# Adding a pooling's two sums to a stored chunk by accumulating transfers from GpSimd

## The reference, cut to what matters

```python
def layer0(x, indices, fc1_w, fc1_b, fc2_w, fc2_b, experts_w, experts_b):
    h = gelu(einsum('bnd,hd->bnh', x, fc1_w) + fc1_b)              # exact gelu
    shared = einsum('bnh,sh->bns', h, fc2_w) + fc2_b               # 384 columns
    expert_x = einsum('bnh,bph->bnp', h, experts_w[indices]) + experts_b[indices][:, None, :]
    return concatenate([shared, expert_x], axis=-1)                # 512 columns

def layer1(hidden, W1, b1, v, prompt_type_ids):
    scores = einsum('bsa,a->bs', tanh(hidden @ W1 + b1), v)
    # per batch: mask l <= j (type 0), l >= j (type 1) or l != j (type 2)
    p = softmax(where(mask, scores[:, None, :], -1e30), axis=-1)
    return einsum('bjl,bld->bjd', p, hidden) / mask.sum(-1)[..., None]

x = x + layer0(x, ...)
x = x + layer1(x, ...)
```

## Time and profile before

| | before |
|---|---|
| median of 3 runs | 1356.64 us (1356.3 to 1356.75) |
| the profiled execution's own time | 1356.64 us |
| its span, first to last instruction | 1354.8 us |
| TensorE busy | 1347.6 us (99%) |
| VectorE busy | 1230.8 us (91%) |
| ScalarE busy | 866.6 us (64%) |
| GpSimd busy | 0.2 us |
| moved by transfers | 62.98 MB |
| mean granted clock of TensorE | 1.000 of full speed |

### The profile page before, as it was taken

One profiled execution on the slowest core, in us unless ns is written; L12 is line 12 of the kernel. 1 busy time (PEld: TensorE's weight loads), 2 busy tenths in 40 slices (PEclk: granted clock), 3 DMA queues, 4 the chain that ended last, 5 costly groups with the idle time before them and its releaser, 6 DMA issues.

```text
span 1354.8 us, 22001 instructions
## 1 busy us (share of the span) xinstructions
PE 1347.6 (99%) x8734; PEld 874.3 (65%) x8734; DVE 1230.8 (91%) x2057; ACT 866.6 (64%) x1493; POOL 0.2 (0%) x4
## 2 busy tenths in 40 slices
PE   9999999999999999999999999999999999999998
PEld 5458476584856758476584756748567584765856
DVE  7988889899898999989899898998989899898998
ACT  4868748376593856848377583756838468483753
POOL 0000000000000000000000000000000000000000
PEclk9999999999999999999999999999999999999999
DMA  8410020110201102011110201102021020200001
GB/s 294 150 48 22 0 71 24 48 48 1 78 17 63 32 8 79 9 62 32 45 50 1 79 17 55 41 0 78 17 63 32 13 77 6 71 24 15 25 10 55
DMA packets 29192, 62.98 MB, mean 46 GB/s; under 512 B 5922, under 2 KB 6690, under 8 KB 26658
## 3 DMA queue, kind: packets, MB, share of 16 engines
q1 hardware_dynamic: 28658, 61.05, 13.7%
q10 hardware_dynamic: 432, 0.53, 0.1%
HBM read 44.79 MB, written 16.78 MB: 45 GB/s over the span
## 4 chain that ended last, share of the span: by engine, by line
PE 96%; DVE 4%; ACT 0%; issue 0%; DVEq 0%
PE ps L398 15%; PE ps L399 15%; PE ps L400 15%; PE ps L317 14%; PE ps L319 14%; PE ps L318 14%; PE ps L430 1%; PE ps L288 1%; PE ps L435 1%; PE ps L598 1%; PE ps L299 1%; PE ps L303 1%; PE ps L301 1%; PE ps L426 1%; PE ps L425 1%; PE ps L424 1%
## 5 line engine op out<-in xcount | busy, mean ns | idle before, releaser
L400 PE MATMUL ps<-hl,w2h 128*128 128x512 f16 x768 | 291.0, 379 | 0.0
L399 PE MATMUL ps<-hh,w2h 128*128 128x512 f16 x768 | 291.0, 379 | 0.0
L398 PE MATMUL ps<-hh,w2l 128*128 128x512 f16 x768 | 291.0, 379 | 0.0
L317 PE MATMUL ps<-xh,w1h 128*128 128x256 f16 x960 | 261.7, 273 | 0.0
L318 PE MATMUL ps<-xl,w1h 128*128 128x256 f16 x960 | 261.7, 273 | 0.0
L319 PE MATMUL ps<-xh,w1l 128*128 128x256 f16 x960 | 261.7, 273 | 0.0
L650 ACT ACTIVATE g<-ps,b1s,ds 128x512 f32<-128x512 f32 x240 | 173.4, 773 | 99.0 <-PE ps L319 99.0
L317 PE MATMUL ps<-xh,ch 128*128 128x256 f16 x720 | 196.4, 273 | 0.0
L319 PE MATMUL ps<-xh,cl 128*128 128x256 f16 x720 | 196.3, 273 | 0.0
L318 PE MATMUL ps<-xl,ch 128*128 128x256 f16 x720 | 196.2, 273 | 0.0
L1064 DVE SCALAR_TENSOR_TENSOR hl<-g,ix,hh 128x512 f16<-128x512 f32 x244 | 179.2, 747 | 1.6
(11 more groups left out here) (208 smaller groups left out, 2348.4 us busy)
## 6 DMA issues: line engine op xcount, KB each, us to landing
xr<-in_xT SPq DMA_DIRECT2D x62, 256.0 KB, 3.1
er<-in_ew SPq DMA_DIRECT2D x15, 1024.0 KB, 6.3
out<-xr SPq DMA_DIRECT2D x60, 256.0 KB, 2.4
raw<-in_w SPq DMA_DIRECT2D x28, 256.0 KB, 6.1
er<-in_w SPq DMA_DIRECT2D x3, 1024.0 KB, 10.1
xr<-in_ew SPq DMA_DIRECT2D x1, 1024.0 KB, 6.2
out<-er SPq DMA_DIRECT2D x3, 256.0 KB, 2.5
xr<-in_xT ACTq DMA_DIRECT2D x2, 256.0 KB, 5.1
```

Source lines behind the costliest of these rows:

```text
L317: mm(to, wh, mh, start=i in (1, 5) and c == 0, stop=False, skip_group_check=True)
L398: mm(po(b, o), wl, hh[:, k, :], start=False, stop=False, skip_group_check=True)
L399: mm(po(b, o), wh, hh[:, k, :], start=False, stop=False, skip_group_check=True)
L400: m = mm(po(b, o), wh, hl[:, k, :], start=False, stop=k == NH - 1, skip_group_check=True)
```

## The change

Of the nine steps of a chunk the last two, the additions on VectorE, are gone, so a batch's pooling has 52 steps. The chunk is stored as soon as it is scaled. GpSimd gets a program: when a chunk's store has landed and the first sum's row is ready, it issues a transfer of this row to the output with an addition in the transfer (511 of the 512 columns, one column shifted), waits until it has landed, and issues the second row's in the same way. Chunks 1 and 3 use the rows `zFi` and `zB` instead of `cp` and `cq`. The products of chunk 2 wait until the transfers of chunk 0 have read their rows (their landing is waited for), those of chunk 3 for chunk 1's; the steps of the next batch's weight rows that write `cp`, `zFi` and `zB` wait for chunks 2 and 3. The counts of `pool` change so that the second layer's part still issues 35 steps, the first layer's part 17 instead of 25; in the tail 47 steps stand ahead of the maxima and none behind the sums.

```diff
--- before.py
+++ after.py
@@ -210,6 +210,8 @@
          "el", "hl", "bound", "sums", "sumsl", "pads", "masks", "combos", "xl", "add0", "add1", "x2l", "awll", "pool",
          "shift", "nl", "scan", "tailmax", "neg", "plow", "pairsum", "wsum", "rz", "outrdy"))
 
+    first_added, second_added = sem("firstadd"), sem("secondadd")
+
 
     def x_loaded(b):
         return 16 * (b // XB + 1)
@@ -262,13 +264,23 @@
     def ds2_value(b, o):
         return 4 + 2 * b - (o == 3) if b else (1, 2, 4, 3)[o]
 
-    ROWS, STEPS = 13, 60
+    ROWS, STEPS = 24, 52
 
     def pool_value(b, step):
         return STEPS * b + step
 
-    def chunk_pooled(b, c):
-        return pool_value(b, ROWS + 11 + 9 * (c + 1))
+    def chunk_scaled(b, c):
+        return pool_value(b, ROWS + 7 * c + 5)
+
+    def first_ready(b, c):
+        return pool_value(b, ROWS + 7 * c + 6)
+
+    def second_ready(b, c):
+        return pool_value(b, ROWS + 7 * c + 7)
+
+    def pooled_rows(c):
+
+        return ((cp, cq), (zFi, zB[:, 0:S]))[c % 2]
 
 
     def tensor_program(eng):
@@ -1212,8 +1224,13 @@
             stt(ga, mBx, cB[:, i], mt, ALU.add, ALU.subtract).then_inc(pool_step)
             yield
             e.wait_ge(io_in, 16)
+            if b:
+                e.wait_ge(first_added, 16 * nth_chunk(b - 1, 2))
             ts(cp, io[:, :], cntq[:, i], cntp[:, i], ALU.mult, ALU.add).then_inc(pool_step)
             yield
+            if b:
+                e.wait_ge(first_added, 16 * nth_chunk(b - 1, 3))
+                e.wait_ge(second_added, 16 * nth_chunk(b - 1, 3))
             if b < LAST - 1:
                 e.wait_ge(exp_done, b + 1)
             else:
@@ -1249,32 +1266,30 @@
             tt(ga, ga, mt, ALU.mult).then_inc(pool_step)
             yield
             for c in range(KD):
-                x, n = chunk(b, c), done + 24 + 9 * c
-                e.wait_ge(pool_step, n - 1 if c else n)
-                tt(cp, wF, x, ALU.mult).then_inc(pool_step)
+                x, n = chunk(b, c), done + ROWS + 7 * c
+                first, second = pooled_rows(c)
+                e.wait_ge(pool_step, n - 7 if c > 1 else n)
+                if c > 1:
+                    e.wait_ge(first_added, 16 * nth_chunk(b, c - 2))
+                tt(first, wF, x, ALU.mult).then_inc(pool_step)
                 yield
-                e.wait_ge(pool_step, n)
-                tt(cq, wB, x, ALU.mult).then_inc(pool_step)
+                if c > 1:
+                    e.wait_ge(second_added, 16 * nth_chunk(b, c - 2))
+                tt(second, wB, x, ALU.mult).then_inc(pool_step)
                 yield
                 e.wait_ge(pool_step, n + 1)
-                scan(cp, aF, cp, 0.0, ALU.mult, ALU.add).then_inc(pool_step)
+                scan(first, aF, first, 0.0, ALU.mult, ALU.add).then_inc(pool_step)
                 yield
                 e.wait_ge(pool_step, n + 2)
-                scan(back_of(cq), back_of(aB), back_of(cq), 0.0, ALU.mult, ALU.add).then_inc(pool_step)
+                scan(back_of(second), back_of(aB), back_of(second), 0.0, ALU.mult, ALU.add).then_inc(pool_step)
                 yield
                 stt(x, be, 1.0, x, ALU.add, ALU.mult).then_inc(pool_step)
                 yield
                 e.wait_ge(pool_step, n + 3)
-                tt(cp[:, 0:S - 1], cp[:, 0:S - 1], al[:, 1:S], ALU.mult).then_inc(pool_step)
+                tt(first[:, 0:S - 1], first[:, 0:S - 1], al[:, 1:S], ALU.mult).then_inc(pool_step)
                 yield
                 e.wait_ge(pool_step, n + 4)
-                tt(cq[:, 1:S], cq[:, 1:S], ga[:, 0:S - 1], ALU.mult).then_inc(pool_step)
-                yield
-                e.wait_ge(pool_step, n + 6)
-                tt(x[:, 1:S], x[:, 1:S], cp[:, 0:S - 1], ALU.add).then_inc(pool_step)
-                yield
-                e.wait_ge(pool_step, n + 8)
-                tt(x[:, 0:S - 1], x[:, 0:S - 1], cq[:, 1:S], ALU.add).then_inc(pool_step)
+                tt(second[:, 1:S], second[:, 1:S], ga[:, 0:S - 1], ALU.mult).then_inc(pool_step)
                 yield
 
         pools = itertools.chain.from_iterable(pooling(b) for b in range(LAST))
@@ -1402,7 +1417,7 @@
 
         for b in range(1, B):
 
-            takes = ((0, 3, 1), (1, 1, 1), (1, 2, 1), (1, 2, 0), (1, 2, 0), (2, 2, 0))
+            takes = ((0, 2, 1), (1, 1, 0), (1, 1, 1), (1, 1, 0), (0, 1, 0), (1, 1, 0))
             if b == 1:
                 takes = ((0, 0, 0),) * 5 + ((1, 1, 1),)
             for c, (one, two, three) in zip(range(2, PAIRS), takes):
@@ -1495,7 +1510,7 @@
         natural_low(1, 1)
         pool(3 + 4 + 3 + 4)
         natural_low(2, 2)
-        pool(4 + 2)
+        pool(2)
         e.wait_ge(score_done, LAST + 1)
         e.wait_ge(own_done, 1)
         scan(mF[:, 1:1 + HALF], pad, pf[3][:, 0:HALF], -BIG, ALU.max, ALU.max).then_inc(scan_step)
@@ -1525,7 +1540,6 @@
         e.wait_ge(pair_sums, 2)
         tt(be, be, mt, ALU.add).then_inc(weights_sum)
         ts(rz[:, :], lcol[:, :], cntq[:, i], cntp[:, i], ALU.mult, ALU.add).then_inc(rz_step)
-        pool(4)
         e.wait_ge(totals_done, 1)
         e.wait_ge(rz_step, 1)
         tt(rz[:, :], pf[0][:, 0:4], rz[:, :], ALU.mult).then_inc(rz_step)
@@ -1562,7 +1576,7 @@
             dma(expert_rows(b), ew[bass.ds(n, 1), :, :].rearrange("a p n -> p (a n)")).then_inc(e_loaded(b)[0], 16)
 
         def store(b, c):
-            e.wait_ge(pool_step, chunk_pooled(b, c))
+            e.wait_ge(pool_step, chunk_scaled(b, c))
             dma(out[b, :, c, :], chunk(b, c)).then_inc(x_out[b % XB * KD + c], 16)
             if b + XB < B:
                 load_x(b + XB, c)
@@ -1614,6 +1628,20 @@
             stores = (B - 1 - i // KD) // XB + 1 + (i == LAST % XB * KD + 3)
             e.wait_ge(s, 16 * stores)
 
+
+    def gpsimd_program(eng):
+        e = Engine(eng)
+        for b in range(LAST):
+            for c in range(KD):
+                first, second = pooled_rows(c)
+                e.wait_ge(x_out[b % XB * KD + c], x_stored(b))
+                e.wait_ge(pool_step, first_ready(b, c))
+                eng.dma_start(out[b, :, c, 1:S], first[:, 0:S - 1], accum_op=ALU.add).then_inc(first_added, 16)
+                e.wait_ge(first_added, 16 * nth_chunk(b, c))
+                e.wait_ge(pool_step, second_ready(b, c))
+                eng.dma_start(out[b, :, c, 0:S - 1], second[:, 1:S], accum_op=ALU.add).then_inc(second_added, 16)
+        e.wait_ge(second_added, 16 * nth_chunk(LAST - 1, 3))
+
     with nc.Block() as block:
         @block.sync
         def _(eng):
@@ -1630,6 +1658,10 @@
         @block.vector
         def _(eng):
             vector_program(eng)
+
+        @block.gpsimd
+        def _(eng):
+            gpsimd_program(eng)
 
 
 def kernel(x, itok_B_0_15, itok_B_0_2, L0_cond_fc1_w, L0_cond_fc1_b, L0_cond_fc2_w, L0_cond_fc2_b,
```

## The result

The changed kernel takes 1390.11 us (median of 6 runs, 1385.36 to 1393.11) against 1356.70 us of the kernel before beside it: ratio 1.0244, 95% interval 1.0228 to 1.026. It is slower by 33 us, where 1357.9 was forecast and 1380 was the end of the range. The profiled execution took 1393.11 us, the slowest of the six, and its span is 1391.3, so what follows is about 36.5 us of span.

What follows compares the result with a forecast made beforehand. TensorE was taken to bound the loop, leaving nothing to gain there. In the tail, 2.67 us less VectorE work against a 4.0 us stall put the scan 1.3 later: 1356.64 + 1.3 = 1357.9 us, range 1355.3 to 1380.

Steps and rivals of the forecast that it cites:

- What bounds the kernel: Loop: TensorE is busy for all 82.00 us of a batch's period, so relieving VectorE there gains nothing.
- What the tail can give: Tail: at most 1.2 us, because the scan ahead of the maxima needs the second half's scores, whose matmuls end at 1332.61.
- The price of one transfer: GpSimd's accumulating transfer: a plain store and two passes more, 4.6 us, between 2.4 and 6.6.
- thresholds of 5.1 and 5.0: Loop: transfer times above which TensorE notices the waits for chunk 0's (5.1 us) and chunk 1's sums (5.0).
- L: Time from the wait that lets GpSimd issue one accumulating transfer to its landing, taken as 4.6 us.
- The upper bound, 6.6: One accumulating transfer: load of the old output, a store and one more pass of the data, 6.6 us in all.
- The wait in the tail: Tail: VectorE stalls 4.0 us once, ahead of chunk 2's second product; the scan before the maxima starts 1.3 us later.
- the rule (2L - 5.2): Tail: VectorE's stall before chunk 2's second product, two transfer times less 5.2 us; 4.0 us at 4.6 each.
- The waits in the loop: Loop: chunks 2 and 3 wait for the transfers of chunks 0 and 1; both hidden at 4.6 us a transfer.
- rival C: Loop: transfers over 5.0 us make chunk 3's second product, behind the expert's load, delay pair 3's `add_second`; 1372 to 1386; 0.36.
- Rival D: Loop: GpSimd's issuing disturbs VectorE, 0.5 us a batch beyond its slack, 7 us, 1364; chance 0.04.
- B: Whole kernel: a transfer costs about a plain store, up to 3.3 us; 1355.4 to 1355.5; chance 0.10.

Runs made afterwards that it cites:

- e1: Changed kernel with rows of its own for each chunk, so no row is reused too early; all 120 transfers stay: 1354.89 us, ratio 0.9985.
- e7: Kernel before, with accumulating transfers and rows of their own only in batch 14's pooling in the tail, eight transfers: 1354.65 us, ratio 0.9984.
- e4: Kernel before, no GpSimd transfers, plus four useless VectorE additions ahead of pair 1's `add_second` in 14 batches: 1391.01 us, ratio 1.0251.
- e3: Changed kernel with the store of chunk 1 ahead of the expert's load in SP's queue: 1384.41 us (one run).
- e5: Kernel with rows of its own for each chunk, but in the loop chunk 3 reuses chunk 1's rows and waits for its transfers: 1365.65 us.
- e6: Kernel with rows of its own for each chunk, but in the loop chunk 2 reuses chunk 0's rows and waits for its transfers: 1378.19 us.
- e2: Changed kernel with the same transfers without the addition, so the sums overwrite what the store left; all waits stay: 1358.2 us (one run).
- e9: Changed kernel with the first sum added on VectorE again before the store, one transfer per chunk instead of two: 1358.51 us, ratio 1.0009.

## Why the prediction was wrong, point by point

**What bounds the kernel: right.** The loop had nothing to give: e1 and e7 have equal times with and without VectorE's relief there, and e4 shows the other half, that lateness at that place is paid in full.

**What the tail can give: right, a little more came.** The bound of 1.2 us was argued from the second half's score, and in e1 TensorE's first matmul with the exponentials starts 1.2 us earlier, counted from the last `stt`. Another 0.4 lies behind TensorE's last matmul (3.1 us to the end in place of 3.6), where I had costed the four steps removed behind the sums at nothing: before, VectorE's last four scalings of 512 columns ran directly behind one another from 1348.56, held up by these steps, and five output transfers were issued within 3 us; in e1 they are spread over 4. That those steps are the cause was not tested by itself. The rest of the 1.9 us of span (2.2 in e7) is 0.2 to 0.5 ahead of the loop.

**The price of one transfer: this is the step that failed.** The term "a plain store and two passes more, 2.4 + 2 x 1.1 = 4.6" measured 6.0 for chunk 0's pair in batches 0 to 12. Its parts were wrong in both directions. The addition costs 1.4 us, not 2.2. GpSimd's queue costs 1.2 over SP's, for which the text said that nothing shows it and gave it nothing. Without company that makes 4.97 us, still under the thresholds of 5.1 and 5.0: batch 13 measures it, and TensorE doesn't wait there. What carried L over the threshold in the other 13 batches is a term that the sum doesn't have: the loads beside the pair, 1.0 us. Chunk 0's store itself sets one of them off, since `load_x` is issued on the same landing 0.3 us ahead of the first transfer, and the expert's 1024 KB follow. The prediction saw that load only in front of chunk 1's store; e3, which takes it away from chunk 0's pair, measures 5.3. Twice L enters the sum and 13 batches multiply it, so 1.4 us too little in one term turned no change into 30 us. The upper bound, 6.6, held the value, but the range's top was taken at 5.8.

**The wait in the tail: right in kind, too small.** The forecast was a stall of 4.0 us and the scan 1.3 later, and it came 4.26 later. The pair's L was 5.5 there, by which the rule (2L - 5.2) gives 5.8; 5.6 were measured ahead of chunk 2's products, and 0.92 more ahead of chunk 3's second, forecast at 0. After its longer wait TensorE's clock was at half for 6.8 us, which cost another 2.1; less the 0.4 above that is the tail's 5.9.

**The waits in the loop: right as a rule, and rival C was what happened, at the other of the two places.** The thresholds were 5.1 for chunk 0's sums and 5.0 for chunk 1's; with L above both, chunk 2's wait comes first in time and pays. By the rule 13 x (2 x 6.0 - 10.2) is 23 us, and 22.2 were waited at pair 1. The slack of "some 1.5 us" behind chunk 2's product was right: a stall of 2.93 left TensorE waiting 1.36, 1.57 less. e5 shows that the wait that I had named costs 11 us by itself, e6 that the other costs 23.5, and e3 that the expert's load matters but as something that lengthens whichever transfers it meets.

**What the sum left out: TensorE's rate after a wait.** After 3 of the 14 waits its granted clock fell to half. The view by stretches of two us, around the third wait (the last three numbers are granted clock, share of the transfer engines, GB/s):

```profile
358.00:360.00 2.00, 0.61 (x6) 0.29 (x3) 2.00 (x2) 0.63 (x2) 0.00 (x0) 1.00 0.99 174
360.00:362.00 2.00, 1.44 (x10) 1.15 (x11) 2.00 (x6) 0.00 (x0) 0.00 (x0) 0.81 0.29 52
362.00:364.00 2.00, 2.00 (x12) 1.37 (x10) 1.97 (x5) 1.30 (x2) 1.08 (x2) 0.50 0.69 151
364.00:366.00 2.00, 2.00 (x17) 1.67 (x16) 0.71 (x2) 1.10 (x4) 0.66 (x1) 0.83 0.92 131
366.00:368.00 2.00, 2.00 (x20) 1.80 (x19) 2.00 (x4) 1.03 (x3) 0.00 (x0) 1.00 1.00 221
```

Between 361 and 365 us the matmuls of 256 columns start every 0.21 us instead of every 0.11, at the lower of the two levels, 1.2 in place of 2.4 GHz; that is worth 1.7 us each time, 5.1 in the loop. Of the other 3.3 us 2.2 are the 0.16 us at each wait, as in e4. Once more in the tail, after the wait of 6.1 us for the first exponentials, it is at half for some 7 us. The prediction priced C by the wait alone: even at L = 6.0 its sum gives 1386. How often the clock falls changes between executions of the changed kernel, with mean clocks of 0.994 to 0.998 and times of 1393.1 to 1385.4. The Trainium skill, TensorE: Matmul & The Clock Gate, section "What's actually happening", says that a gate halves the array's clock according to how busy it has been; by that rule, the trace agrees, a wait can cost more than its length.

**Rival D fell, and B.** e1 has all the transfers, no lost time, and `add_second` at 0.43 us as before. B needed L up to 3.3; even the plain transfers of e2 have 3.57 with no load beside them, and land 3.1 us after their issue where nothing runs beside them, against the prediction's estimate of 2.6.

## What to carry to other kernels

Before work is moved off an engine, ask what the bounding engine waits for: if it waits for nothing, the relief is worth nothing and each new wait is at full price. An accumulating transfer takes work off VectorE but is long in latency, and two in a row were 12 us here; give it a buffer that nobody needs until it has landed, or keep one of the two sums on the engine. Price a transfer in the company it will have: look for what the other queue issues on the same landing. And when a term is bounded by 2.4 and 6.6, valued at 4.6, and a loop multiplies whatever lies above 5.0, the likeliest case is not a safe one.

## What was not expected of the hardware

- A plain transfer of 256 KB issued by GpSimd took 3.1 us from its issue to landing with nothing beside it (e2, median of 36) and 3.9 beside a load of x, where SP's stores take 2.4; with the addition it took 4.8 alone (median of 24 in the changed kernel), 5.3 beside a load of x and 5.65 beside that and the expert's. GpSimd's next issue began 0.28 to 0.36 us after a landing, SP's 0.02.
- The packets of an accumulating transfer took 1.98 us of all 16 engines' time against 0.67 without the addition. A plain store of 256 KB issued while one was under way took 4.4 us to land in the median of e3, and up to 6.2.
- In the loop TensorE's clock fell after waits of 1.95, 2.27 and 2.62 us in the changed kernel and after one of 1.97 in e6. It did not fall after one of 1.93 in the changed kernel, 14 of 1.84 or 1.85 in e4, 2.12 and 2.29 in e6 and 2.81 in e3. In the tail it fell after 2.5 us in e9 and not after 2.9 in e2. The length of the wait alone doesn't decide it; what does was not tried.
